# Moving three pairs of small products among the sixteen builds of a spectral step

## What is computed

```python
x = x + _L0_conv_ref(_gn(x), L0_conv_f)      # upsample by 2, leaky relu, downsample by 2
x = x + _L1_conv_ref(_gn(x), ...)            # spectral convolution
```

```python
o1  = einsum('jxk,ky,bcxy->jbcxy', c, d, x_ft)
out = einsum('oi,icj,jbcxy->boxy', a, b, o1)
```

## Time and profile before

| what | value |
|---|---|
| median of 3 runs | 5586.66 us |
| the profiled execution, its own time | 5585.79 us |
| its span, first to last instruction | 5583.7 us |
| instructions in the span | 209051 |
| mean granted TensorE clock | 0.962 |
| busy: TensorE matmul / VectorE / ScalarE / GpSimd | 89% / 77% / 61% / 46% |
| middle stage, first to last remainder `Ml` | 3243.6 to 5070.8 us |

### The profile page before, as it was taken

The page is one execution under the profiler, slowest core; times in us unless marked ns, Lnnn a source line. Parts: engine busy times, 40 slices in busy tenths (PEclk is TensorE's granted clock), DMA queues, the critical chain, the costliest instruction groups (busy, mean ns, idle before and its releaser), DMA issues. The chain is left out here.

```text
span 5583.7 us, 209051 instructions
## 1 busy us (share of the span) xinstructions
PE 4973.1 (89%) x83616; PEld 4383.9 (79%) x83616; DVE 4280.4 (77%) x6708; ACT 3399.0 (61%) x6347; POOL 2560.3 (46%) x2565
## 2 busy tenths in 40 slices
PE   8989989989989899899899469988998998888999
PEld 6877777778777777787778468888888888888999
DVE  7878878868878788788787588888888888884333
ACT  6756757757657567577576056666666666663332
POOL 6746747747647567477475033333333333330000
PEclk9999999999999999999999589999999999999999
DMA  1131132131131221311312312222222222226999
GB/s 54 50 92 57 51 92 59 51 92 50 55 93 51 85 66 51 92 59 49 94 48 61 106 61 67 68 75 75 75 75 75 71 68 72 75 75 235 420 421 399
DMA packets 606618, 553.41 MB, mean 99 GB/s; under 512 B 14900, under 2 KB 540084, under 8 KB 589364
## 3 DMA queue, kind: packets, MB, share of 16 engines
q1 hardware_dynamic: 606132, 546.48, 29.6%
HBM read 277.99 MB, written 268.44 MB: 98 GB/s over the span
## 5 line engine op out<-in xcount | busy, mean ns | idle before, releaser
L1154 DVE TENSOR_TENSOR Ml<-ring,Mh 128x1024 f16<-128x1024 f32 x1024 | 1199.1, 1218 | 200.3 <-ACT Mh L1121 192.5
L244 POOL TENSOR_TENSOR Y<-Yf,Y 128x532 f16<-128x532 f32 x1024 | 1210.3, 1195 | 132.0 <-ACT Y L478 89.7
L1121 ACT ACTIVATE Mh<-ring 128x1024 f16<-128x1024 f32 x1024 | 986.4, 1022 | 319.5 <-PE ring L1055 319.0
L1055 PE MATMUL ring<-wcur,b_hi 64*128 64x128 f16 x16384 | 747.6, 217 | 204.3 <-DVE Ml L1154 137.7
L278 PE MATMUL ring<-uth,A 128*128 128x266 f16 x6144 | 822.6, 284 | 33.6 <-issue 17.5
L1055 PEld LDWEIGHTS ring<-wcur,b_hi 64*128 64x128 f16 x16384 | 609.3, 94 | 275.0 <-DVE Ml L1154 155.2
L659 DVE TENSOR_TENSOR Yf<-ring,L 128x532 f32<-128x532 f32 x1024 | 686.4, 706 | 117.2 <-ACT L L474 105.7
L278 PEld LDWEIGHTS ring<-uth,A 128*128 128x128 f16 x6144 | 615.4, 100 | 195.3 <-issue 30.4
L1055 PE MATMUL ring<-wcur,b_lo 64*128 64x128 f16 x8192 | 715.1, 216 | 0.0
L237 POOL CAST Y<-Yf 128x532 f16<-128x532 f32 x512 | 320.6, 626 | 724.7 <-DVE Yf L659 724.3
L474 ACT ACTIVATE L<-ring 128x532 f32<-128x532 f32 x1024 | 603.0, 605 | 60.2 <-PE ring L278 49.7
(11 more groups left out here) (139 smaller groups left out, 9823.0 us busy)
## 6 DMA issues: line engine op xcount, KB each, us to landing
xb<-in_x SPq DMA_DIRECT2D x128, 512.0 KB, 4.2
x<-x1b SPq DMA_DIRECT2D x64, 1024.0 KB, 6.7
spec<-sp_out SPq DMA_DIRECT2D x256, 256.0 KB, 2.6
xin<-spec SPq DMA_DIRECT2D x128, 512.0 KB, 6.4
fd<-ft SPq DMA_DIRECT2D x128, 512.0 KB, 4.5
F<-fd SPq DMA_DIRECT2D x64, 1024.0 KB, 20.0
xq<-x SPq DMA_DIRECT2D x64, 1024.0 KB, 16.8
out<-yq SPq DMA_DIRECT2D x64, 1024.0 KB, 18.5
```

The costliest lines, as they stand in the source:

```text
L244: pool.tensor_tensor(Y[:, e, 1, m], Yf[:, m], Y[:, e, 0, m], ALU.subtract).then_inc(e_yl, 1)
L1055: mm = pe.matmul(ring[:, UNIT_PAIR[n], t, 128 * k:128 * k + 128], b[r, z, 4 * u + k, :], wcur[r, z, w, :], start=(part == 0), stop=(part = ...
L1121: act.activation(hi, ps, ACT.Copy).then_inc(e_hi, 1)
L1154: dve.tensor_tensor(lo, ps, hi, ALU.subtract).then_inc(e_lo, 1)
```

## The change

Three of the six places in a step move. Before, pairs of groups stood behind units 3 and 5 (app1), 7 and 9 (out), 11 and 14 (app0). After, they stand behind units 2 and 4 (app1), 7 and 9 (out), 12 and 15 (app0). The number of builds, of groups and of instructions stays the same, as do the semaphores and the values that are waited for. Since TensorE, ScalarE and VectorE read the same tuples, the order changes in all three queues alike.

```diff
--- before.py
+++ after.py
@@ -45,7 +45,7 @@
 UNIT_PAIR = (0, 1, 2) * 5 + (1,)
 AUX = 3
 YQ = 16
-APP1_AT, OUT_AT, APP0_AT = (3, 3, 5, 5), (7, 7, 9, 9), (11, 11, 14, 14)
+APP1_AT, OUT_AT, APP0_AT = (2, 2, 4, 4), (7, 7, 9, 9), (12, 12, 15, 15)
 ROWS = 4
```

## The result

The changed kernel takes 5608.17 us, the median of 7 runs (5605.52 to 5614.27), against 5586.66 us before (7 runs, 5573.56 to 5598.26). The ratio is 1.0041, with a 95% interval of 1.0028 to 1.0053. The kernel became slower by 0.4%, where 0.5% faster was forecast. The profiled execution took 5613.26 us.

The account below looks back on a forecast made before the run. Waits between TensorE and VectorE in the middle stage were taken as the bound. A step of 28.19 in place of 28.68 us saves 30.4 us over 62 steps: 5585.79 to 5555.4, stated as 5557 us, range 5547 to 5581.

Parts of the forecast that it names:

- The pieces of a step: Builds, apply pairs, remainders and evictions timed from one traced step, re-added in the new order: 28.19 us, before 28.68.
- Unit 15, unit 1, the second app1 pair: TensorE's waits for VectorE: 2.07 us ahead of unit 15, 0.05 at unit 1, some 0.5 at the second app1 pair.
- The total of the waits for the remainder: TensorE's waits for VectorE's remainders in the middle stage: to stay near 132 us, gathered in one place.
- The loop's turn: Loop turn between the second app0 pair and unit 0, taken to cost some 0.07 us; bounds 0 and 0.5 us.
- The second rival: Loop turn fetches from memory, nearest price 2.6 us: about 2.0 us a step, 124 us, 5711 us; chance 0.05.
- the treatment of the clock: TensorE in the middle stage: full clock assumed in every step, busy share rising to 25.90 in 28.19 us.
- the sum: Middle stage: each step 0.49 us shorter, 30.4 us over 62 steps, 5557 us in all; chance 0.73.
- the third rival: TensorE's clock falls as its longest wait grows from 1.65 to 2.07 us: 161 us, 5748 us; chance 0.02.
- The forecast's own sign: Unit 0 on TensorE starts 9.80 us after unit 10; a start later than 10.2 refutes the forecast.

Follow-up runs that it names:

- the added wait: Kernel before, order kept, with unit 15 waiting for the remainder of unit 14 in place of unit 13: 5714.29 us, ratio 1.0232.
- the split one: Changed kernel with the third app0 group behind unit 14 and only the fourth behind unit 15: 5546.4 us, ratio 0.992.

## Why the prediction was wrong

**The pieces of a step held, with one exception.** A step at full clock took 28.32 us (28.19 forecast) in the changed kernel, 28.03 (28.03) with app1 alone, 29.82 (29.83) with the added wait, 27.82 (27.8 to 28.0) in the split one and 27.60 (27.4 to 27.5) with app0 behind 13 and 15. With app0 alone it took 29.51 (28.85 to 28.98), because the wait of unit 3 was overlooked.

**Unit 15, unit 1, the second app1 pair**: right. 1.98 us of waiting at unit 15 in place of 2.07. In the short step nothing to speak of is left at unit 1, and the wait at the second app1 pair stays. The total of the waits for the remainder came to 127.1 us, forecast near 132.

**The loop's turn**: mis-sized by a little. From the start of unit 15 to unit 0 the forecast had 9.80 - 7.32 = 2.48 us; it is 3470.33 - 3467.71 = 2.62. Some 0.05 of the 0.14 us stands between unit 15 and the pair, 0.09 at the turn itself, which cost 0.16 in place of 0.07. This goes nearly one for one to the end of the step, as the forecast said a loss there would (28.32 against 28.19), 8 us in all. The second rival, a stall of 2.6 us at the turn, didn't come; its threshold was also mis-added: a turn of 0.8 us would have cost 0.2% by the forecast's own terms, 62 x (0.8 - 0.07 - 0.05 - 0.49), not over 0.3%.

What the Trainium skill says in "Runtime: NRT & Kernel Launch", section "Instruction fetch mechanics", on a forced fetch behind a taken branch shows in no run here; the turn cost 0.16 us.

**The step that failed** is the treatment of the clock: the sum took a full clock for granted in every step, and the third rival, which doubted it, was put aside with this sentence: "Against: its busy share rises from 25.90 in 28.70 to 25.90 in 28.19, at a clock of 1.00". I read the clock's safety from TensorE's share over a whole step. The share did rise, and the total of its waits did fall. But the waits gathered in one place: 0.51 and 1.65 us with 1.44 us of building between them became one of 1.98 with the rest gone. The clock fell in 55 of 62 steps, each time behind that place. The long steps have a mean of 29.09 us, so one fall costs 29.09 - 28.32 = about 0.77 us, 55 of them 42 us. The order's own gain was 62 x 0.36 = 22 us. The difference, 20 us of loss, is what 62 steps of 29.01 in place of 28.68 us give, and the measured medians lie 21.5 us apart. The forecast's own sign shows it too: unit 0 was to start at 9.80 us after unit 10, and a start later than 10.2 was to refute the sum. In the short step it starts at 9.92, in the long one at 3528.20 - 3517.95 = 10.25. I had the rival's mechanism, but gave it 2 chances in 100, and a net loss of 161 us, priced from a stretch of another stage, where TensorE stood still far more. That the wait was the cause is shown from both sides: filling it returns the 42 us, and adding waits to the old order brings the falls without moving anything.

What stays open is what exactly lets the clock fall. The runs give an order, not a law. Counted by the 62 steps, with the main waits of an undisturbed one:

- before, 0.51, 1.65 and 0.52 us: no fall;
- the gap filled with two products, 0.52, 0.86 and 0.52: 2 falls;
- the late order (app0 behind 13 and 15), 0.19 and 1.07: 7;
- the split order, 0.52, 0.50 and 0.58: 11;
- the changed kernel, 1.98 and 0.52: 55;
- the added wait, 1.64, 1.58 and 0.52: 59.

The first has longer waits and more of them in all than the three below it (2.68 us against 1.90, 1.26 and 1.60), and more in all than the changed kernel (2.50). So neither the longest wait nor the sum over the step orders them. How close the waits stand to each other, and what work lies between and behind them, was not separated. That narrow products count less than wide ones near a wait would fit the split and the late order, but in the filled gap they did as well, so it is only a guess.

The Trainium skill, in "TensorE: Matmul & The Clock Gate", section "A second HAM failure mode: psum-queue depth-cycling", says that an engine that stands still briefly and often between groups of matmuls, as it cycles through its PSUM buffers, can lose its clock again and again. The traces agree in part: 0.95 over the middle stage of the changed kernel, but 1.00 before, where TensorE also stands still three times a step. The rule names the danger and doesn't tell the two orders apart; weighed in the forecast, it would have spoken for a larger chance than 0.02.

## What to carry to other kernels

Once a step is worked out piece by piece from one trace, moves of whole groups can be forecast to 0.2 us, if each build's wait is followed in the new order; one that was overlooked cost 0.5 us. Look then at where the remaining waits of TensorE end up, not at their sum. If an order gathers them in one place, price a fall of the clock there, and put something into the gap: real work first, a few useless products second. An idle engine that nobody waits for may still be worth keeping busy, and the clock is to be asked for by stretch, since a digit of the page hides a loss of 5%.

## What the runs showed of the hardware

- Two useless products (0.6 us of a 2.0 us wait) cut the falls of the clock from 55 steps to 2; six, or fifty narrow ones, to none.
- A fall costs less than its half speed suggests. In the long step above TensorE was busy 3.24 us of 3.30 at a clock of 0.51, which is, by an estimate from this row, 1.6 us of work lost; the long steps grew by 0.7 to 0.9 us. Part of the loss presumably lay where TensorE would have waited for VectorE; with the added wait, the wait ahead of unit 1 shrinks from 1.58 us to 1.13 behind a fall. In the other kernels a fall cost 0.6 to 0.9 us, and 1.8 us in about every fourth step of the one with the added wait, where it lasted twice as long.
- The steps that were spared in the changed kernel came regularly, every tenth: the short one from 3453.69 us on, the next from 3743.84, then 4033.95. In the split kernel the ones that were hit came regularly, every fifth or sixth, in the late order every eighth or ninth. The waits of all these steps are alike, so something besides the step's own work decides whether a wait lets the clock fall. The regular spacing suggests its place in time; no run moved it.
